# First stage of a four-layer graph network: scores earlier in TensorE's step, output projection two steps behind in fp32r parts

## The chip, the cores and the metric

The kernel runs on one core of one Trainium2 chip. The metric is the device time of one execution in microseconds. Engines named here: TensorE (PE, matrix products into PSUM banks), VectorE (DVE), ScalarE (ACT), GpSimd (POOL) and SyncE (SP, which issues the DMAs).

## The reference

Four graph layers over x [64, 128, 256] with one adjacency matrix of 128 x 128. Only the first matters here, attention with 8 heads of 32:

```python
h = jnp.maximum(_layernorm(x, axis=-1), 0.0)
q = split_heads(h @ Wq.T + bq)
k = split_heads(h @ Wk.T + bk)
v = split_heads(h @ Wv.T + bv)
scale = 1.0 / np.sqrt(D_HEAD)
scores = jnp.einsum('bhqd,bhkd->bhqk', q, k) * scale
scores = jnp.where(mask, -jnp.inf, scores)        # mask: adj == 0
attn = jax.nn.softmax(scores, axis=-1)
out = jnp.einsum('bhqk,bhkd->bhqd', attn, v)
x = x + out.transpose(0, 2, 1, 3).reshape(b, n, D_MODEL) @ Wo.T + bo
```

## The kernel before

The 64 graphs are taken in 32 groups of two (G = 2), and x stays in SBUF from the first layer to the last. Each layer is a stage of its own: a software pipeline over the groups, written by hand as one function per engine (`step0` to `step3`). `run_steps` calls such a function for steps -2, -1, 0, ... (the first and last ones written out, the middle in a hardware loop of two steps), and `at.group(lag)` gives the group that an engine handles in this step at a lag: `f` is the step's own group g, `b` the one before it, `n` the one after it. The order in each engine's queue is the order of the code; semaphores alone tie the engines together.

In a step of the first stage TensorE does, in this order: the q and k projections of group g (each 12 products of 256 columns, the inputs split into a high and a low fp32r part, three products for each pair, L1172); the transposes T0 and T1 of the first two blocks of probabilities of group g-1 (L1195; block r holds four heads' rows); the values of g (L1180); T2 and T3; the transposes of the normalised h of g+1 (L1160); the four mask products that fill banks 4 to 7 with -3e38 where there is no edge (L1224); the transposes of the widened reciprocal sums (L1229); the attention products of g-1 (32 short ones, L1237); the scores of g, added on the mask (L1246); and the output projection of g-1 in fp32 (L1259).

Bank 0 holds hT and the k projection, bank 1 the q projection and the values, bank 2 the transposes T0 and T2 and then the attention, bank 3 T1, T3, the sums and the output projection, banks 4 to 7 the scores. VectorE adds the k bias (kT, L591), copies T1 and T3 (L584), takes LayerNorm's statistics and moments for g+2 (L246, L261), the reciprocals (L602, L606), the low part hT_lo (L613), the attention times the reciprocals (att0T, L620), the four negated maxima (L625) with a small scaling behind each (L628), and adds the projection into x (L638). In steps 0 to 3 it also does a `late_part` each at the end of the step, weight preparation for later layers (L555 to L573), each instruction of which waits for the one before. ScalarE adds the q bias (L904), takes the exponentials (L894), copies T0 and T2 (L887), the values (L916) and the sums (L928), rounds hT_hi (L923) and normalises h (L289). GpSimd turns moments into scale and shift (L273 to L279) and adds the output bias into x (L302).

## Time and profile before

| | |
|---|---|
| median of 3 runs | 1662.28 us (1660.25 to 1665.63) |
| the profiled execution | 1662.14 us, its span 1660.3 us |
| TensorE, VectorE, ScalarE, GpSimd busy | 89%, 77%, 62%, 27% of the span |
| mean granted clock of TensorE | 0.965 of 2.4 GHz |
| first stage, last add into x ends | 459.4 us |

The span is counted from the first to the last instruction of the profiled execution. A timeline row gives start, length, engine, line and operation, what it writes and reads, and how often it stands there in a row; a bracket at its end is the idle time of the engine just before it, with what ended it. "PEclk" is the clock granted to TensorE, 1.00 for 2.4 GHz and 0.50 for 1.2 GHz. Matrix products overlap, so the distance from start to start is what one costs; the length of a row also holds the end of the last one. An fp32 product is recorded as two passes, so the four products of the output projection stand there as x8.

### The profile page before, as it was taken

The page shows a single profiled execution, that of the slowest core. Times are in us where ns is not written, and L with a number is a line of the kernel's source. Part 1 is how long each engine was busy: PE and PEld are TensorE (multiplying, and loading weights), DVE is VectorE, ACT ScalarE, POOL GpSimd, SP SyncE. Part 2 cuts the span into 40 slices and gives each one's busy share as a digit, 9 for nine tenths or more (in the row PEclk, how much of TensorE's full clock was granted, in tenths as well). Part 3 has the DMA queues.
Part 4 walks back from the last instruction along what each step waited for, and adds up shares of the span by engine and source line. Part 5 has one row for each costly group of instructions (what it writes and reads, how often), then busy time and mean ns, then how long its engine had stood idle before and what let it go on. Part 6 is the DMA issues. An engine that isn't in the chain of part 4 may idle for free.

```text
span 1660.3 us, 36159 instructions
## 1 busy us (share of the span) xinstructions
PE 1471.5 (89%) x11454; PEld 1242.8 (75%) x11517; DVE 1283.4 (77%) x3002; ACT 1021.6 (62%) x3208; POOL 440.7 (27%) x745
## 2 busy tenths in 40 slices
PE   5789999999879977999999999999999999975776
PEld 4678888888779965787877777787877778764554
DVE  4877777777567758788888888888888888754997
ACT  3568788788645546565666556565666656533776
POOL 1112212212046642031222223132222222122332
PEclk9899999999979988999999999999999999996999
DMA  7400000000000000000000000000000000000112
GB/s 235 133 2 0 0 0 0 0 0 0 1 1 0 0 0 1 1 1 1 0 0 0 0 0 0 0 0 0 0 0 0 0 0 1 1 1 7 64 63 70
DMA packets 23873, 24.22 MB, mean 15 GB/s; under 512 B 1936, under 2 KB 23184, under 8 KB 23696
## 3 DMA queue, kind: packets, MB, share of 16 engines
q1 hardware_dynamic: 23824, 23.60, 4.5%
q8 instruction: 26, 0.43, 0.1%
q14 instruction: 23, 0.19, 0.0%
HBM read 15.21 MB, written 8.39 MB: 14 GB/s over the span
## 4 chain that ended last, share of the span: by engine, by line
PE 42%; DVE 26%; ACT 18%; issue 11%; POOL 1%; DVEq 0%; DMA 0%; ACTq 0%; SPq 0%; POOLq 0%
ACT probs L894 9%; PE bank L1323 4%; PE bank L1436 4%; PE bank L1160 3%; DVE headsT_lo L695 3%; PE bank L1374 3%; DVE probs L706 3%; PE bank L1246 2%; DVE em L688 2%; PE bank L1389 2%; PE bank L1237 2%; ACT probs L1005 2%; PE bank L1278 2%; PE bank L1290 2%; PE bank L1291 2%
## 5 line engine op out<-in xcount | busy, mean ns | idle before, releaser
L894 ACT ACTIVATE probs<-bank,negtop 128x128 f32<-128x128 f32 x512 | 185.8, 415 | 47.6 <-DVE negtop L628 47.5
L273 POOL TENSOR_TENSOR var_eps<-mv,eps_tile 128x2 f32<-128x2 f32 x128 | 38.3, 299 | 636.6 <-DVE mv L261 636.6
L1330 PE MATMUL bank<-aggT_hi,wh_hi 128*128 128x256 f32 x512 | 148.5, 290 | 12.2 <-DVE em L690 9.2
L289 ACT ACTIVATE h<-x_all,shift,rstd 128x256 f32 (+1 forms) x256 | 139.9, 596 | 31.5 <-POOL shift L279 31.5
L1343 PE MATMUL bank<-wout_hi,headsT_hi 128*128 128x258 f32 x512 | 156.2, 305 | 0.0
L980 ACT CAST aggT_hi<-bank 128x512 fp32r<-128x512 f32 x128 | 75.2, 588 | 120.3 <-PE bank L1323 120.3
L1330 PE MATMUL bank<-aggT_lo,wh_hi 128*128 128x256 f32 x512 | 145.1, 283 | 0.0
L1330 PE MATMUL bank<-aggT_hi,wh_lo 128*128 128x256 f32 x512 | 145.1, 283 | 0.0
L1343 PE MATMUL bank<-wout_lo,headsT_hi 128*128 128x258 f32 x512 | 144.5, 282 | 0.0
L1343 PE MATMUL bank<-wout_hi,headsT_lo 128*128 128x258 f32 x512 | 144.2, 282 | 0.0
L1323 PE MATMUL bank<-probsT,h 128*128 128x512 f32 x256 | 133.2, 625 | 0.5 <-ACT probsT L1013 0.5
L894 ACT ACTIVATION_READ_ACCUMULATOR probs<-bank,negtop 128x1 f32 x512 | 130.1, 254 | 0.0
L485 POOL TENSOR_TENSOR var_y<-mv_y,eps_tile 128x2 f32<-128x2 f32 x32 | 6.3, 196 | 466.3 <-DVE mv_y L755 466.3
L695 DVE TENSOR_TENSOR headsT_lo<-em,headsT_hi 128x512 fp32r<-128x512 f32 x128 | 127.6, 1014 | 2.7 <-ACT headsT_hi L993 2.4
L993 ACT CAST headsT_hi<-em 128x512 fp32r<-128x512 f32 x128 | 79.1, 618 | 61.8 <-DVE em L690 61.8
L1330 PEld LDWEIGHTS bank<-aggT_hi,wh_hi 128*128 128x128 f32 x512 | 97.4, 190 | 19.4 <-DVE em L690 15.6
L275 POOL TENSOR_TENSOR rstd<-var_eps,pow_half 128x2 f32<-128x2 f32 x128 | 104.6, 817 | 10.0
L701 DVE TENSOR_TENSOR aggT_lo<-bank,aggT_hi 128x512 fp32r<-128x512 f32 x128 | 86.6, 677 | 24.2 <-ACT aggT_hi L980 24.1
L1195 PE MATMUL bank<-consts,probs 128*128 128x128 f32 x512 | 75.7, 281 | 31.7 <-DVE probsT L584 17.1
L1160 PE MATMUL bank<-consts,h 128*128 128x128 f32 x384 | 64.6, 295 | 43.0 <-ACT h L289 43.0
L1005 ACT ACTIVATE probs<-probs,negtop 128x128 f32<-128x128 f32 x256 | 99.4, 400 | 1.0 <-DVE negtop L708 1.0
L1343 PEld LDWEIGHTS bank<-wout_lo,headsT_hi 128*128 128x128 f32 x512 | 97.3, 190 | 1.0 <-issue 0.2
(209 smaller groups left out, 4718.2 us busy)
## 6 DMA issues: line engine op xcount, KB each, us to landing
x_all<-in_x SPq DMA_DIRECT2D x32, 256.0 KB, 2.8
out_x<-x_all SPq DMA_DIRECT2D x32, 256.0 KB, 2.1
wh<-in_L_gnn_W_heads SPq DMA_DIRECT2D x2, 512.0 KB, 7.7
a_heads<-in_L_gnn_a_heads SPq DMA_DIRECT2D x1, 1024.0 KB, 11.0
wout<-in_L_gnn_W_out SPq DMA_DIRECT2D x1, 1024.0 KB, 11.1
raw<-in_L_gnn_W SPq DMA_DIRECT2D x1, 512.0 KB, 5.6
ffn<-in_L_gnn_w SPq DMA_DIRECT2D x2, 256.0 KB, 7.1
consts<-in_shape_consts SPq DMA_DIRECT2D x1, 322.0 KB, 2.7
```

What stands on the lines that cost most here:

```text
L275: nc.gpsimd.tensor_tensor(rstd[:, p, :], var_eps[:, p, :], pow_half[:, :], ALU.pow).then_inc(s.norm, 1)
L289: last = nc.scalar.activation(h[:, p, c, :], x_all[:, bass.ds(g * G + c, 1), :].rearrange("p a d -> p (a d)"), ACT.Relu, bias=shift[:, p, ...
L695: nc.vector.tensor_tensor(headsT_lo[:, i].rearrange("p k c n -> p k (c n)"), em[:, i % 2], headsT_hi[:, i].rearrange("p k c n -> p k (c n) ...
L701: nc.vector.tensor_tensor(aggT_lo[:, dc, :, c, :], bank[3 + (2 + i) % 4][:, :].rearrange("p (h n) -> p h n", h=H2), aggT_hi[:, dc, :, c, : ...
L894: last = nc.scalar.activation(probs[:, r, i, :], bank[4 + r][:, i * N:(i + 1) * N], ACT.Exp, bias=negtop0[:, r, i:i + 1], scale=float(DH) ...
L993: nc.scalar.copy(headsT_hi[:, i].rearrange("p k c n -> p k (c n)"), em[:, i % 2]).then_inc(hd2_hi, 1)
L1005: last = nc.scalar.activation(probs[:, c, hh, :], probs[:, c, hh, :], ACT.Exp, bias=negtop2[:, c, hh:hh + 1], accum_out=sum2[:, c, hh:hh + 1])
L1160: last = nc.tensor.transpose(dst[:, (k * G + c) * N:(k * G + c + 1) * N], src[:, c, k * N:(k + 1) * N], ident)
L1195: last = nc.tensor.transpose(bank[2 + r % 2][:, k * N:(k + 1) * N], probs[:, r, k, :], ident)
L1323: nc.tensor.matmul(bank[3 + (2 + i) % 4][:, :], h[:, pm, c, dc * N:(dc + 1) * N], probsT[:, c].rearrange("p h n -> p (h n)"), start=True, ...
L1330: last = nc.tensor.matmul(bank[3 + i % 2][:, o * G * N:(o + 1) * G * N], w[:, k, i, o * N:(o + 1) * N], src[:, k, i].rearrange("p c n -> p ...
L1343: last = nc.tensor.matmul(bank[5 + c][:, 0:D + 2], src[:, i, o, c, :], w[:, k, :], start=(k == 0 and src is headsT_hi and w is wout_hi), s ...
```

## The change

- **Scores.** The mask products and the scores of g move from the end of TensorE's step to the place behind T0, T1 and T2, ahead of the values. VectorE's maxima 0 to 2 move up with them, the fourth goes near the end of VectorE's step; ScalarE takes exponentials 0, 1 and 2 in this step and the fourth in the next.
- **Output projection.** It handles group g-2 (`z`, lag 2) between the two halves of the k projection, writes bank 2, and is made of three fp32r products for each pair, out of att0T_hi, att0T_lo and woT_hi, woT_lo. VectorE makes att0T_hi and att0T_lo in each step, and the weights' parts once in the setup. The add into x is the first thing in VectorE's step, for g-2.
- **Scale.** The factor 32^-0.5 goes into q's activation (and into bq once), out of the exponential and out of the small scaling behind each maximum, which is dropped.
- **Third bank for transposes.** T2 goes to bank 1, T0, T1, T2 stand together, and T3 goes to bank 2 behind h's transposes; ScalarE copies T0 and T2, VectorE T1 and T3.
- **h.** ScalarE normalises h of g+1 in the step, not of g+2; the statistics for g+2 stand behind the attention on VectorE.

```diff
@@ block.vector, setup
+            nc.vector.tensor_scalar(bq_c[:, :], bq_c[:, :], float(DH) ** -0.5, None, ALU.mult)
...
+            nc.vector.tensor_copy(woT_hi[:, :, :], bank[3][:, :].rearrange("p (c o) -> p c o", c=2)).then_inc(weights_dve, 1)
+            dve.wait_ge(weights_dve, 6)
+            nc.vector.tensor_tensor(woT_lo[:, :, :], bank[3][:, :].rearrange("p (c o) -> p c o", c=2), woT_hi[:, :, :].bitcast(FP32),
+                                    ALU.subtract).then_inc(weights_dve, 1)
@@ block.vector, step0
+                if z:
+                    dve.wait_ge(o_full, gz + 1)
+                    dve.wait_ge(pre[0].bias, gz + 1)
+                    nc.vector.tensor_tensor(x_group(gz), bank[2][:, :].rearrange("p (c d) -> p c d", c=G), x_group(gz),
+                                            ALU.add).then_inc(pre[0].x, 1)
...
+                    nc.vector.tensor_tensor(att0T[:, :, :, :], bank[2][:, :].rearrange("p (k c n) -> p k c n", k=KC, c=G),
+                                            rsumT[:, :, :, :], ALU.mult).then_inc(aT_ready, 1)
+                    dve.wait_ge(aT_ready, gb * 3 + 1)
                     if positive(gb):
                         dve.wait_ge(o_full, gb)
-                    nc.vector.tensor_tensor(att0T[:, :, :, :], bank[2][:, :].rearrange("p (k c n) -> p k c n", k=KC, c=G),
-                                            rsumT[:, :, :, :], ALU.mult).then_inc(aT_ready, 1)
...
-                    dve.wait_ge(top0_step, g * 8 + 2 * r + 1)
-                    nc.vector.tensor_scalar(negtop0[:, r, :], negtop0[:, r, :], float(DH) ** -0.5, None, ALU.mult).then_inc(top0_step, 1)
...
+                    nc.vector.tensor_copy(att0T_hi[:, :, :, :], att0T[:, :, :, :]).then_inc(aT_ready, 1)
+                    dve.wait_ge(aT_ready, gb * 3 + 2)
+                    nc.vector.tensor_tensor(att0T_lo[:, :, :, :], att0T[:, :, :, :], att0T_hi[:, :, :, :].bitcast(FP32),
+                                            ALU.subtract).then_inc(aT_ready, 1)
+                pre_dve(dve, 0, at)
+                stats_written(dve, 0, at)
+                if f:
+                    top(3)
+                moments_dve(0, at)
@@ block.scalar, step0
                 if b:
-                    exp(2, gb, pb)
+                    exp(3, gb, pb)
                     probs_T(0)
-                    exp(3, gb, pb)
+                    probs_T(2)
@@ block.tensor, step0
                     project_T(bank[1], wqT_hi, wqT_lo).then_inc(q_full, 1)
-                    project_T(bank[0], wkT_hi, wkT_lo).then_inc(k_full, 1)
+                    project_T(bank[0], wkT_hi, wkT_lo, (0,))
+                if z:
+                    pe.wait_ge(aT_ready, gz * 3 + 3)
+                    for c in range(G):
+                        for k in range(KC):
+                            for src, w in ((att0T_hi, woT_hi), (att0T_hi, woT_lo), (att0T_lo, woT_hi)):
+                                last = nc.tensor.matmul(bank[2][:, c * D:(c + 1) * D], src[:, k, c, :], w[:, k, :],
...
-                if b:
-                    pe.wait_ge(aT_ready, gb + 1)
-                    for c in range(G):
-                        for k in range(KC):
-                            last = nc.tensor.matmul(bank[3][:, c * D:(c + 1) * D], att0T[:, k, c, :], woT[:, k, :],
-                                                    start=(k == 0), stop=(k == KC - 1))
-                    last.then_inc(o_full, 1)
```

On TensorE the order of one step (of those written out at the front), the first row of a group each (T1 left out in the second), is before:

```order
L1195 MATMUL bank2<-consts,probs 128x128 [waits aT_ready,p0_ready]
...
L1195 MATMUL bank3<-consts,probs 128x128 [waits x_done0,p0_ready]
...
L1180 MATMUL bank1<-wvT_hi,hT_hi 128x256 [waits q_ready]
...
L1195 MATMUL bank2<-consts,probs 128x128 [waits pT0_act,p0_ready]
...
L1195 MATMUL bank3<-consts,probs 128x128 [waits pT0_dve,p0_ready]
...
L1160 MATMUL bank0<-consts,h 128x128 [waits k_ready,h0]
...
L1224 MATMUL bank4<-hide0,ident_bf 128x512 [waits p0_ready]
...
L1229 MATMUL bank3<-consts,rwide0 128x128 [waits pT0_dve,rsum0_step]
...
L1237 MATMUL bank2<-probsT,v1 32x128 [waits pT0_act,v_ready]
...
L1246 MATMUL bank4<-kT,qT 128x128 [waits k_ready]
...
L1259 MATMUL bank3<-woT,att0T 128x256 [waits aT_ready]
...
L1172 MATMUL bank1<-hT_hi,wqT_hi 128x256 [waits v_ready,hT0_lo]
```

and after (line numbers of the changed kernel: L1184 projections, L1231 output projection, L1207 probabilities, L1245 masks, L1215 scores, L1192 values, L1171 h, L1276 attention):

```order
L1184 MATMUL bank1<-hT_hi,wqT_hi 128x256 [waits v_ready,hT0_lo]
...
L1231 MATMUL bank2<-woT_hi,att0T_hi 128x256 [waits aT_ready]
...
L1184 MATMUL bank0<-hT_hi,wkT_hi 128x256
...
L1207 MATMUL bank2<-consts,probs 128x128 [waits x_done0,p0_ready]
...
L1207 MATMUL bank1<-consts,probs 128x128 [waits q_ready,p0_ready]
...
L1245 MATMUL bank4<-hide0,ident_bf 128x512 [waits p0_ready]
...
L1215 MATMUL bank4<-kT,qT 128x128 [waits q_ready,k_ready]
...
L1192 MATMUL bank1<-wvT_hi,hT_hi 128x256 [waits pT0_act]
...
L1171 MATMUL bank0<-consts,h 128x128 [waits k_ready,h0]
...
L1207 MATMUL bank2<-consts,probs 128x128 [waits pT0_act,p0_ready]
...
L1266 MATMUL bank3<-consts,rwide0 128x128 [waits pT0_dve,rsum0_step]
...
L1276 MATMUL bank2<-probsT,v1 32x128 [waits pT0_dve,pT0_act,v_ready]
```

The masks and scores have moved from behind the attention to ahead of the values, and T3 from ahead of h's transposes to behind them; the sums' transposes and the attention products follow T3 directly. The output projection, once the last group of the step, stands between the halves of the k projection, and T0, which now waits for the add into x (x_done0), comes behind it.

On VectorE the same part of a step is before:

```order
L591 TENSOR_SCALAR kT<-bank0,bk_c 128x256 [waits s0_full,k_full,late_setup]
...
L584 COPY probsT<-bank3 128x512 [waits av_full,pT0_full]
L246 BN_STATS st<-x_all 128x6 [waits x_loaded1]
...
L602 RECIPROCAL rsum0<-sum0 128x16 [waits rT_full,p0_ready,stats0]
L261 BN_AGGR mv<-st 128x2 x2
L606 TENSOR_SCALAR rwide0<-rsum0,poison 128x512 [waits rsum0_step]
L584 COPY probsT<-bank3 128x512 [waits pT0_full]
L613 TENSOR_TENSOR hT_lo<-bank0,hT_hi 128x512 [waits hT0_hi]
L620 TENSOR_TENSOR att0T<-bank2,rsumT 128x512 [waits o_full,rT_ready,av_full]
L625 TENSOR_REDUCE negtop0<-bank4 128x4 [waits s0_full,p0_ready]
L628 TENSOR_SCALAR negtop0<-negtop0 128x4 [waits top0_step]
...
L638 TENSOR_TENSOR x_all<-bank3,x_all 128x512 [waits bias0,o_full]
```

and after (L602 the add into x, L609 kT, L592 copies of T1 and T3, L596 maxima, L633 hT_lo, L638 att0T):

```order
L602 TENSOR_TENSOR x_all<-bank2,x_all 128x512 [waits bias0,o_full,late_setup]
L609 TENSOR_SCALAR kT<-bank0,bk_c 128x256 [waits s0_full,k_full]
...
L592 COPY probsT<-bank3 128x512 [waits av_full,pT0_full]
L617 RECIPROCAL rsum0<-sum0 128x16 [waits rT_full,p0_ready]
L619 TENSOR_SCALAR rwide0<-rsum0,poison 128x512 [waits rsum0_step]
L596 TENSOR_REDUCE negtop0<-bank4 128x4 [waits s0_full,p0_ready]
...
L592 COPY probsT<-bank2 128x512 [waits pT0_full]
L633 TENSOR_TENSOR hT_lo<-bank0,hT_hi 128x512 [waits hT0_hi]
L638 TENSOR_TENSOR att0T<-bank2,rsumT 128x512 [waits rT_ready,av_full]
L643 CAST att0T_hi<-att0T 128x512 [waits o_full,aT_ready]
L645 TENSOR_TENSOR att0T_lo<-att0T,att0T_hi 128x512 [waits aT_ready]
L248 BN_STATS st<-x_all 128x6 [waits x_loaded1]
```

The add into x has gone from the end of the step to its front, where it waits for the projection (o_full) and stands ahead of kT. The maxima stand ahead of the copy of T3, and two more operations, att0T_hi and att0T_lo, follow att0T ahead of the statistics (BN_STATS).

## Rows read from the trace of the kernel before

**Rows 1.** Busy time of each engine in one window, a steady step.

```profile
core 0: us, PE busy (x) PEld busy (x) DVE busy (x) ACT busy (x) POOL busy (x), PEclk, DMA share, GB/s
232.40:244.80 12.40, 11.96 (x137) 10.64 (x137) 8.79 (x21) 10.02 (x42) 2.78 (x5) 1.00 0.00 0
```

**Rows 2.** Waits from 108 to 404 us: total us, times, longest us.

```profile
PE bank L1195 <- ACT probs L894: 9.3, 24, 0.4
```

**Rows 3.** Timeline of TensorE, one steady step: start us, us, what it runs.

```profile
232.39 0.47 PE L1172 MATMUL bank<-hT_hi,wqT_hi 128*128 128x256 f32 x1
232.69 0.28 PE L1172 MATMUL bank<-hT_hi,wqT_lo 128*128 128x256 f32 x1
...
235.44 1.04 PE L1195 MATMUL bank<-consts,probs 128*128 128x128 f32 x8
236.23 0.36 PE L1180 MATMUL bank<-wvT_hi,hT_hi 128*128 128x256 f32 x1
...
237.75 0.60 PE L1195 MATMUL bank<-consts,probs 128*128 128x128 f32 x4
238.74 0.66 PE L1195 MATMUL bank<-consts,probs 128*128 128x128 f32 x4 [0.39 <-ACT probs L894]
239.23 0.60 PE L1160 MATMUL bank<-consts,h 128*128 128x128 f32 x4
...
240.53 0.60 PE L1229 MATMUL bank<-consts,rwide 128*128 128x128 f32 x4
241.06 1.08 PE L1237 MATMUL bank<-probsT,v 128*32 128x128 f32 x32
242.07 1.17 PE L1246 MATMUL bank<-kT,qT 32*128 32x128 f32 x32
243.17 1.99 PE L1259 MATMUL bank<-woT,att0T 128*128 128x256 f32 x8
244.82 0.47 PE L1172 MATMUL bank<-hT_hi,wqT_hi 128*128 128x256 f32 x1
```

**Rows 4.** Timeline of VectorE, the same step.

```profile
243.26 0.69 DVE L625 TENSOR_REDUCE negtop<-bank 128x4 f32<-128x512 f32 x1 [0.36 <-PE bank L1246]
...
244.09 0.69 DVE L625 TENSOR_REDUCE negtop<-bank 128x4 f32<-128x512 f32 x1
...
248.96 0.68 DVE L584 COPY probsT<-bank 128x512 f32<-128x512 f32 x1
```

**Rows 5.** Line 638, the add into x: count, then minimum, median, maximum in ns.

```profile
L638 DVEq FUSED_REGOPS  x26: 71/71/71, 109.8 to 420.6; - x26
```

**Rows 6.** Timelines of VectorE and TensorE in steps 2 and 3, around a late part.

```profile
61.86 0.88 DVE L591 TENSOR_SCALAR kT<-bank,bk_c 128x256 f32<-128x256 f32 x2
...
72.93 0.69 DVE L638 TENSOR_TENSOR x_all<-bank,x_all 128x512 f32<-128x512 f32 x1
73.53 0.68 DVE L563 TENSOR_TENSOR prod<-wh,a_heads 128x512 f32<-128x512 f32 x1
...
79.32 0.88 DVE L591 TENSOR_SCALAR kT<-bank,bk_c 128x256 f32<-128x256 f32 x2
...
80.94 1.09 PE L1195 MATMUL bank<-consts,probs 128*128 128x128 f32 x4 [3.76 <-DVE probsT L584]
```

**Rows 7.** Windows behind TensorE's restart in step 3.

```profile
80.90:82.90 2.00, 1.94 (x8) 1.85 (x10) 1.93 (x7) 0.00 (x0) 0.90 (x2) 0.50 0.00 0
84.90:86.90 2.00, 2.00 (x64) 1.69 (x64) 0.69 (x1) 1.57 (x3) 0.15 (x1) 1.00 0.03 8
```

**Rows 8.** Lines 688 and 695, second GNN stage: minimum, median, maximum in ns.

```profile
L688 DVE TENSOR_SCALAR em<-em x128: 411/420/1123, 644.2 to 1462.9; 128x512 f32<-128x512 f32 x128
...
L695 DVE TENSOR_TENSOR headsT_lo<-em,headsT_hi x128: 676/682/1790, 647.0 to 1465.6; 128x512 fp32r<-128x512 f32 x128
```

**Rows 9.** Timeline of VectorE in the setup.

```profile
18.01 0.42 DVE L536 TENSOR_TENSOR bo_row<-bank,bo_row 128x256 f32<-128x256 f32 x1 [0.44 <-PE bank L1152]
```

**Rows 10.** Timeline of TensorE, end of the first stage.

```profile
454.87 3.78 PE L1259 MATMUL bank<-woT,att0T 128*128 128x256 f32 x8 [0.81 <-DVE att0T L620]
```

More of the change, by code:

```diff
@@ L183, in build_program @@
                 woT = sb_0("woT", [N, KC, D])
+                woT_hi, woT_lo = [sb_0(f"woT_{part}", [N, KC, D], F32R) for part in ("hi", "lo")]
                 hT_hi = sb_0("hT_hi", [N, KC, G, N], F32R)
@@ L190, in build_program @@
                 att0T = sb_0("att0T", [N, KC, G, N])
+                att0T_hi, att0T_lo = [sb_0(f"att0T_{part}", [N, KC, G, N], F32R) for part in ("hi", "lo")]
             with ExitStack() as layer1:
@@ L1166, in step0, with project_T @@
                 b, gb, pb = at.group(1)
-                def project_T(dst, w_hi, w_lo):
-                    for o in range(KC):
+                z, gz, _ = at.group(2)
+                def project_T(dst, w_hi, w_lo, parts=(0, 1)):
+                    for o in parts:
                         for k in range(KC):
@@ new lines, in step0 @@
+                if f:
+                    project_T(bank[0], wkT_hi, wkT_lo, (1,)).then_inc(k_full, 1)
+                if b:
+                    probs_T(0)
+                    probs_T(1)
+                    probs_T(2)
+                if f:
+                    for r in range(4):
+                        if positive(g):
+                            pe.wait_ge(p0_ready, g * 4 - 3 + r)
+                        nc.tensor.matmul(bank[4 + r][:, :], ident_bf[:, :], hide0[:, :, :], start=True, stop=False)
@@ new lines, in step0 @@
+                if b:
+                    pe.wait_ge(v_ready, gb + 1)
+                    pe.wait_ge(pT0_act, gb * 2 + 2)
+                    pe.wait_ge(pT0_dve, gb * 2 + 2)
+                    for k in range(KC):
+                        for c in range(G):
+                            i = k * G + c
+                            for r in range(4):
+                                last = nc.tensor.matmul(bank[2][r * DH:(r + 1) * DH, i * N:(i + 1) * N], v1[:, pb, c, k * 4 + r, :],
+                                                        probsT[:, r, i, :], start=True, stop=True)
+                    last.then_inc(av_full, 1)
```

147 lines of the change are left out of this document (62 added, 85 removed).

## The prediction

> **What bounds the kernel now.** The change touches the first stage alone, the attention layer, which runs from the setup to 459.4 us. I read it in this order. First one step in windows: in 12.40 us TensorE is busy for 11.96, ScalarE for 10.02, VectorE for 8.79, at the full granted clock of 2.4 GHz [rows 1]. So TensorE's own work nearly fills the step. Then the waits of 24 steps: TensorE waits in one place for another engine, for the exponentials ahead of the transpose of the fourth block of probabilities, 9.3 us in all, 0.39 a step [rows 2]. Then its timeline gives the step: 232.39 to 244.82, that is 12.43 us, cut into pieces by the starts of the groups [rows 3]. Two things should be seen there. A 256-column fp32r product follows the one before it after 0.12 us (23 of them from 232.69 to 235.44); the first behind fp32 work takes 0.30. And the four fp32 products of the output projection (eight passes) take 1.65. Last the steps of the fill: VectorE has a late part to do in steps 0 to 3 (weight preparation of later layers, 5.8 us in step 2), and the steps there are 17.46 us long, from one kT to the next (61.86 to 79.32) [rows 6].
>
> **TensorE's own work after.** The projection becomes 12 fp32r products in the middle of fp32r work: 12 x 0.12 = 1.43 instead of 1.65, a gain of 0.22. The wait of 0.39 ahead of T3 goes: T3 now stands behind scores and values, long after the fourth exponential. T2 took 0.99 with that wait, 0.60 without; in one row of transposes it should take 0.40, as T0 and T1 do (0.79 for both), a gain of 0.20. T3 takes 0.49 after its wait and should take 0.40, and the transposes of the sums behind it 0.40 instead of 0.53 (the mask products no longer stand in front). The first q product now follows the short attention products, not the fp32 projection, about -0.10. The scores inherit the place behind the mask products, +0.09. Sum: 12.43 - 0.22 - 0.39 - 0.20 - 0.09 - 0.13 - 0.10 + 0.09 = 11.39 us, if nothing waits.
>
> **What is late next, in the steady steps.** Two waits come in, by the order of after and the durations of before. (1) T0 writes bank 2, which the projection of two steps back has just filled, so T0 waits for VectorE's add into x. The projection's last product ends 0.16 behind the next issue (0.28 against 0.12 in [rows 3]), the semaphore takes 0.03 (243.24 to 243.26 from the scores to the first maximum [rows 3, 4]), VectorE's address registers for x_all come behind the wait and take 0.07 in the loop [rows 5], the add is 0.69 [rows 6], 0.06 more on both sides: 1.01. The second half of the k projection covers 0.71. Wait 0.30, and 0.1 for the restart (T3 shows 0.49 against 0.40). (2) The attention products need the fourth block copied by VectorE. T3's end, 0.16 + 0.03, the copy 0.68 [rows 4], 0.03: 0.90, of which the sums' transposes cover 0.40. Wait 0.50. Step: 11.39 + 0.40 + 0.50 = 12.29, say 12.3 us. Against 12.43 this is -0.13, and over 27 steady steps -3.5 us.
>
> **VectorE and ScalarE in the steady step.** VectorE loses four scalings: maximum to maximum is 0.83 [rows 4], to become 0.61, so -0.9. It gains the copy att0T_hi and the difference att0T_lo. Neither is in the trace. For the difference the nearest row is headsT_lo, two SBUF sources of 128x512, median 0.68, maximum 1.79 [rows 8]; I take 0.69. For the copy the nearest is the one-source operation on em in SBUF, median 0.42 [rows 8]; the other end is 0.69, as a copy out of PSUM takes. I take 0.43. Then from the end of the attention products: 0.14, multiply 0.69, copy 0.43, difference 0.69 and two gaps of 0.04, that is 2.06 us into the next step, and TensorE wants it at 1.53 + 0.71 = 2.24. Covered by 0.18; with the copy at 0.69 a wait of 0.08. Behind them stand the statistics, the fourth maximum and the moments, which end near 3.4, before the projection does (3.8). The Trainium skill, VectorE: DVE Perf Modes, section "The perf-mode tier table", gives an fp32 tensor_copy in SBUF the double rate and a tensor_tensor the single one; by that rule the sum stays as it is, and if the copy fell out of it (0.69) some 2 us would be added. No row here shows whether an fp32r output keeps the double rate. ScalarE has the same work in another order; its next maximum is there before it is free, or it waits 1.2 us with nothing behind that TensorE needs. The scale folded into q costs nothing there, since the same instruction carries it. The normalised h is made one step later than before, at about 6.5 us into the step, for transposes at 9.4.
>
> **The fill.** This is where the change loses. Setup: two more operations with PSUM sources, 0.6 each from start to start (as 72.93 to 73.53 [rows 6]), and the small scaling of bq on VectorE, less the 0.44 that it idles there now [rows 9]: +0.8. In steps 2, 3 and 4 the add into x will be the first thing on VectorE, behind the late part of the step before. Today kT comes there and TensorE's T3 waits 3.76 us for the next copy [rows 6]; then it works at 1.2 GHz for some 3 to 4 us (clock 0.50 in the window from 80.90, 1.00 in that from 84.90 [rows 7]). After the change the chain from the late part is: add 0.6; T0, T1, T2 at the low clock 2.4 to 2.6; masks 1.3 to 1.7; scores 1.1; that is 5.6. Then values, h's transposes and T3 2.4, tail 0.2, copy 0.7, attention products 1.1, multiply, copy and difference 1.8, statistics, fourth maximum and moments 1.5: 13.3 us ahead of the next late part. Today it is 17.46 less the late part (73.53 to 79.32, 5.8) = 11.7. So +1.6 in each of two steps and half as much in the one behind step 3: +4. Steps 0 and 1 I take as even, since there is no projection yet.
>
> **The drain.** At half clock the last projection takes 3.78 [rows 10], twice what it takes in the steady step; as 12 fp32r products at twice 0.12 it takes 2.9. The copy and difference in front of it cost 1.2, its gain is 0.9: even, within the 1 us or so that the other waits there may shift.
>
> **Sum.** -3.5 + 0.8 + 4 + 0 = +1.3 us on the profiled execution's 1662.14 (span 1660.3), which stands at the median of the runs, 1662.28. I forecast 1663 us. Within 0.3%, 5 us, is what a measurement of this kernel can't tell from no change.
>
> **Rivals.** (A) Faster: the waits cost less than I put on them, or TensorE's groups lie closer. For it speaks that the bare work falls to 11.39 and VectorE's idle time is ample (3.6 us of 12.4). Each 0.1 us less of a step is 2.7 us; with the two waits at 0.5 instead of 0.9 the step is 11.9, -0.53 x 27 = -14, and with setup and fill at +5 the time is 1653. Against it: both waits are chains of known operations. Chance 0.25. (B) Slower, by the difference att0T_lo. The nearest operations mostly take 0.68, but some take up to 1.79 [rows 8]. If the difference takes 1.0 here, by whatever holds those up, and the copy 0.69, the chain is 2.61 instead of 2.06, TensorE waits 0.4 for the projection, and the step is 12.7: 27 x 0.27 = +7, with setup and fill +5 and their own four steps +2: 1676. It decides from a chain of 2.2 us on. Against it: GpSimd's norm and bias work starts when the moments are done, near 3.4 us into the step, when the difference is over. Chance 0.13. The Trainium skill, SBUF — State Buffer, section "Who interferes with whom", has the rule behind it: a VectorE instruction with two SBUF inputs and a GpSimd one that reads SBUF exclude each other for the whole instruction; it would give this rival's time only if the two overlap. (C) Slower, by the clock in the fill. After a late part TensorE restarts today with eight transposes and four masks, and the clock is back within some 4 us of the restart (0.50, then 1.00, [rows 7]). After the change it restarts with 12 transposes, later in VectorE's chain; if the clock comes back later there, scores and values run at 1.2 GHz too, 1.1 + 1.5 us more in each of three steps at the worst, 1671, and 1667 at the half. For it speaks only that the idle time ahead is longer, 5 us against 3.76. Chance 0.12. (D) The change does what it says and the gain and the loss cancel: my forecast, 0.50, its own range 1657 to 1668.
>
> **Range and chances.** The step may be 12.1 to 12.5 (-9 to +2), the fill and setup +3 to +7, the drain -1 to +2. With the rivals the range is 1652 to 1673. Faster by over 0.3%: 0.25 (A). Within: 0.51. Slower by over 0.3%: 0.24 (B, most of C and a little of D).
>
> **What would show it.** In the steady steps of after: a period of 12.3; T0 waiting about 0.3 for x_all; the attention products waiting about 0.5 for probsT; the projection's 12 products in 1.43 us with no wait ahead of them; att0T_hi at 0.43. In steps 2 and 3: a period near 19 us, with TensorE idle for 5 us ahead of T0. The prediction is wrong if the attention products don't wait, or if the fill's steps stay near 17.5 us.

## The result: 0.9% slower

The changed kernel takes 1678.08 us (median of 4 runs, 1676.88 to 1679.08) against 1663.95 us for the kernel before on the same chip. The ratio is 1.0088, its 95% interval 1.0066 to 1.0109. I had forecast 1663 us and a range up to 1673.

Nearly the whole of it lies in the first stage. In the profiled executions its last add into x ends at 475.06 us instead of 459.38; what follows takes 1201.7 us instead of 1200.9. Cut at the kT of steps 0, 5 and 31, from VectorE's timeline:

| stretch | before | after | difference | forecast |
|---|---|---|---|---|
| start to kT of step 0 | 30.14 | 31.61 | +1.5 | +0.8 |
| kT 0 to kT 5 (fill) | 81.31 | 89.04 | +7.7 | +4 |
| kT 5 to kT 31 (26 steady steps) | 323.08 | 330.25 | +7.2 | -3.4 |
| kT 31 to the last add's end (drain) | 24.85 | 24.16 | -0.7 | 0 |

The steady steps, as a window of one of them (us; busy time of TensorE, its weight loads, VectorE, ScalarE, GpSimd; granted clock) and as TensorE's waits from 108 to 404 us. This is the view of [rows 1, 2]:

```profile
242.04:254.73 12.69, 11.93 (x139) 10.61 (x141) 9.39 (x20) 10.15 (x42) 2.51 (x5) 1.00 0.00 0
```

```profile
PE bank L1276 <- ACT v L938: 10.1, 23, 0.4
PE bank L1207 <- DVE x_all L602: 6.6, 23, 0.3
PE bank L1245 <- issue: 0.2, 1, 0.2
```

The period is 12.71 us (mean of the 20 steps from kT 8 to kT 28, as everywhere below), where it was 12.43. TensorE's busy time has not moved (11.93, was 11.96), and the one wait of 0.39 has become two, of 0.44 and 0.29. The view puts the first down to ScalarE's v. Its timeline and VectorE's correct that:

```profile
251.29 0.39 PE L1192 MATMUL bank<-wvT_hi,hT_hi 128*128 128x256 f32 x1
...
252.82 0.60 PE L1171 MATMUL bank<-consts,h 128*128 128x128 f32 x4
253.26 0.60 PE L1207 MATMUL bank<-consts,probs 128*128 128x128 f32 x4
253.69 0.60 PE L1266 MATMUL bank<-consts,rwide 128*128 128x128 f32 x4
254.73 1.08 PE L1276 MATMUL bank<-probsT,v 128*32 128x128 f32 x32 [0.44 <-ACT v L938]
```

```profile
243.18 0.69 DVE L638 TENSOR_TENSOR att0T<-bank,rsumT 128x512 f32<-128x512 f32 x1 [0.69 <-PE bank L1276]
243.90 0.43 DVE L643 CAST att0T_hi<-att0T 128x512 fp32r<-128x512 f32 x1
244.36 0.69 DVE L645 TENSOR_TENSOR att0T_lo<-att0T,att0T_hi 128x512 fp32r<-128x512 f32 x1
...
253.89 0.69 DVE L592 COPY probsT<-bank 128x512 f32<-128x512 f32 x1 [0.63 <-PE bank L1207]
```

The attention products need the v of a step ago (the code waits for `gb + 1`), which was copied long before. VectorE's copy of T3 ends at 253.89 + 0.69 = 254.58, 0.15 ahead of them: that is the wait I had foreseen. In a_scale, one of the experiments below, the same view names that copy (probsT, 10.1 us, 23 times) and not v. The other place, T0 behind the output projection, in the same step:

```profile
245.30 0.28 PE L1231 MATMUL bank<-woT_hi,att0T_hi 128*128 128x256 f32 x1
...
246.74 0.28 PE L1184 MATMUL bank<-hT_hi,wkT_hi 128*128 128x256 f32 x1
...
247.34 0.28 PE L1184 MATMUL bank<-hT_lo,wkT_hi 128*128 128x256 f32 x1
...
247.89 1.50 PE L1207 MATMUL bank<-consts,probs 128*128 128x128 f32 x12 [0.27 <-DVE x_all L602]
```

The 12 fp32r products take 246.74 - 245.30 = 1.44 us and nothing waits ahead of them. T0 starts 0.55 behind the last k product instead of 0.12, so its wait costs 0.43 with the restart.

The fill, in the view of [rows 6]: VectorE and GpSimd at the end of step 1 with the start of the next late part, and TensorE's restart in step 3 (the first of its four mask products is missing in the record):

```profile
60.44 0.69 DVE L571 TENSOR_REDUCE wh_f<-prod 128x2 f32<-128x512 f32 x1
61.16 1.33 DVE L570 TENSOR_TENSOR prod<-wh,a_heads 128x512 f32<-128x512 f32 x1
...
78.34 0.66 DVE L570 TENSOR_TENSOR prod<-wh,a_heads 128x512 f32<-128x512 f32 x1
```

```profile
60.68 1.26 POOL L304 TENSOR_TENSOR x_all<-x_all,bo_row 128x512 f32<-128x512 f32 x1
```

```profile
85.57 2.79 PE L1207 MATMUL bank<-consts,probs 128*128 128x128 f32 x12 [6.12 <-DVE x_all L602]
88.59 1.06 PE L1245 MATMUL bank<-hide,ident_bf 128*128 128x512 bf16 x3 [0.22 <-issue]
89.58 1.17 PE L1215 MATMUL bank<-kT,qT 32*128 32x128 f32 x32
```

TensorE idles for 6.12 us ahead of T0 (3.76 in [rows 6]) and restarts at half clock: 3.02 us from T0 to the first recorded mask product. One operation of the late part takes 1.33 us instead of 0.69: it starts while GpSimd adds the output bias (60.68 to 61.94), and ends 0.55 behind it. The same happens in step 2 (81.20, beside an addition from 80.72 to 81.98).

### The profile page after: what moved, and what is told of

Its sections match the earlier page's. It is cut to its first block, busy times and chain, and to the rows that moved or that the text cites. A ratio compares the mean times of both kernels' runs of the same rounds, so it can differ in the third digit from the quotient of the medians.

```text
span 1676.8 us, 36577 instructions
## 1 busy us (share of the span) xinstructions
PE 1468.7 (88%) x11582; PEld 1241.9 (74%) x11645; DVE 1304.4 (78%) x2941; ACT 1024.1 (61%) x3208; POOL 437.3 (26%) x745
## 4 chain that ended last, share of the span: by engine, by line
PE 48%; DVE 28%; ACT 12%; issue 10%; POOL 1%; DVEq 1%; DMA 0%; SPq 0%; ACTq 0%; POOLq 0%
PE bank L1340 4%; PE bank L1184 4%; PE bank L1453 4%; DVE headsT_lo L707 3%; PE bank L1391 3%; PE bank L1207 3%; PE bank L1231 3%; PE bank L1171 3%; DVE probs L718 3%; ACT probs L906 2%; PE bank L1215 2%; DVE em L700 2%; PE bank L1406 2%; PE bank L1276 2%; PE bank L1309 2%
## 5 line engine op out<-in xcount | busy, mean ns | idle before, releaser
L906 ACT ACTIVATE probs<-bank,negtop 128x128 f32<-128x128 f32 x512 | 182.2, 400 | 64.5 <-DVE negtop L596 64.5
L275 POOL TENSOR_TENSOR var_eps<-mv,eps_tile 128x2 f32<-128x2 f32 x128 | 33.9, 265 | 655.6 <-DVE mv L263 655.6
L906 ACT ACTIVATION_READ_ACCUMULATOR probs<-bank,negtop 128x1 f32 x512 | 122.3, 239 | 0.0
L596 DVE TENSOR_REDUCE negtop<-bank 128x4 f32<-128x512 f32 x128 | 82.5, 686 | 38.1 <-PE bank L1215 34.8
L1171 PE MATMUL bank<-consts,h 128*128 128x128 f32 x384 | 62.3, 287 | 43.8 <-ACT h L291 43.8
```

The source lines that it names most:

```text
L596: nc.vector.tensor_reduce(negtop0[:, r, :], bank[4 + r][:, :].rearrange("p (k n) -> p k n", k=4), AX.X, ALU.max, negate=True).then_inc(top ...
L906: last = nc.scalar.activation(probs[:, r, i, :], bank[4 + r][:, i * N:(i + 1) * N], ACT.Exp, bias=negtop0[:, r, i:i + 1], accum_out=sum0[: ...
L1171: last = nc.tensor.transpose(dst[:, (k * G + c) * N:(k * G + c + 1) * N], src[:, c, k * N:(k + 1) * N], ident)
```

## The experiments

Twelve kernels besides the changed one; the fill is from kT 0 to kT 5 as in the table above. The ratio is to the kernel before on the same chip. Fill and step come from one profiled execution each.

| kernel | us | ratio (95% interval) | fill | steady step |
|---|---|---|---|---|
| after | 1678.1 | 1.0088 (1.0066 to 1.0109) | 89.0 | 12.71 |
| a_late | 1670.8 | 1.0048 (1.0032 to 1.0064) | 59.0 | 12.71 |
| b_late | 1662.6 | 1.0005 (0.9994 to 1.0015) | 58.6 | 12.43 |
| a_t3 | 1665.8 | 1.0020 (1.0008 to 1.0032) | 89.5 | 12.31 |
| a_t1t3 | 1654.0 | 0.9944 (0.9923 to 0.9965) | 86.9 | 11.86 |
| a_nobias | 1678.1 | 1.0113 (1.0093 to 1.0134) | 88.0 | 12.71 |
| a_proj32 | 1681.2 | 1.0130 (1.0111 to 1.0149) | 88.4 | 13.06 |
| a_scale | 1683.2 | 1.0142 (1.0121 to 1.0164) | 92.0 | 12.80 |
| a_bank | 1688.1 | 1.0170 (1.0148 to 1.0192) | 91.4 | 13.17 |
| a_split | 1662.5 | 1.0018 (1.0006 to 1.0030) | 76.2 | 12.71 |
| b_split | 1651.6 | 0.9949 (0.9929 to 0.9968) | 71.4 | 12.41 |
| a_t1t3s | 1637.8 | 0.9862 (0.9841 to 0.9883) | 73.9 | 11.86 |
| a_best | 1634.0 | 0.9845 (0.9827 to 0.9864) | 74.7 | 11.83 |

The rest of the program behind the first stage took between 1198.5 and 1204.6 us in these profiles (1226.6 and 1223.6 in a_late and b_late, which do the late parts there), so differences of 3 us between single times say little; the periods say more.

**The two waits: a_t3 and a_t1t3.** T3 goes ahead of h's transposes:

```diff
                     values(1).then_inc(v_full, 1)
+                if b:
+                    probs_T(3)
                 n, gn, pn = at.group(-1)
 ...
                     transpose_group(bank[0], h[:, pn]).then_inc(hT0_full, 1)
                 if b:
-                    probs_T(3)
                     pe.wait_ge(rsum0_step, gb * 2 + 2)
```

> The changed kernel with the transpose T3 ahead of h's transposes instead of behind them, so that h's transposes (0.44 us) too lie between T3 and the attention products. Theory (the attention products wait some 0.5 us for VectorE's copy of T3, and this wait is on the path of the steady step): the wait goes, 0.4 to 0.5 us a step, the period falls from 12.71 to 12.25 to 12.35 us, and the whole takes 11 to 13 us less than the changed kernel, about 1666. Rival (the step is set by a loop through VectorE or ScalarE, and TensorE's waits are only where the slack shows): the wait moves to another group, to h's transposes or the next q projection, and the period stays above 12.6.

The period fell by 0.40, to 12.31, so the rival, a loop through another engine, is out. In a_t1t3 T1 stands ahead of T0 too (with the counts of pT0_full that the others wait for):

```diff
                 if b:
-                    probs_T(0)
                     probs_T(1)
+                    probs_T(0)
                     probs_T(2)
```

> As a_t3, and T1 ahead of T0 as well, since T1 goes to bank 3 and needs no add into x. Theory: T1 (0.44 us) covers the wait for the add too (0.4 us with the restart), and the step is TensorE's bare work of some 11.8 us; the whole is 22 to 25 us less than the changed kernel, about 1654, which is below the kernel before. Rival (a loop through VectorE): VectorE now starts the copy of T1 before kT, no gain over a_t3, or less than 0.1 us a step.

Another 0.45: the period is 11.86, and the change with its two waits covered beats the kernel before. TensorE's timeline of one step, which is now its bare work:

```profile
241.18 0.60 PE L1207 MATMUL bank<-consts,probs 128*128 128x128 f32 x4
241.61 0.60 PE L1171 MATMUL bank<-consts,h 128*128 128x128 f32 x4
242.05 0.60 PE L1267 MATMUL bank<-consts,rwide 128*128 128x128 f32 x4
242.65 1.08 PE L1277 MATMUL bank<-probsT,v 128*32 128x128 f32 x32
243.66 0.38 PE L1184 MATMUL bank<-hT_hi,wqT_hi 128*128 128x256 f32 x1
...
248.10 1.51 PE L1207 MATMUL bank<-consts,probs 128*128 128x128 f32 x12
249.45 1.03 PE L1245 MATMUL bank<-hide,ident_bf 128*128 128x512 bf16 x4
```

T0 to T2 take 1.35 us, T3 and h's transposes 0.44 each, and the sums' transposes 0.60, with no wait recorded. I had put 1.19, 0.40 and 0.40 on T0 to T2, T3 and the sums. The restart costs more than the idle time that the waits' view shows for it: T0's wait stands there with 0.29, and covering it brought 0.45.

**The fill: a_late and b_late.** In both kernels the four late parts go behind the first stage:

```diff
-                if isinstance(at.t, int) and 0 <= at.t < 4:
-                    late_part(at.t)
             run_steps(dve, NG, step0)
+            for i in range(4):
+                late_part(i)
```

> The changed kernel with its four late parts taken out of steps 0 to 3 and done in a row behind the first stage. Read from kT of step 0 to kT of step 5: the kernel before has 81.3 us there, the changed one 89.0; five steady steps of the changed kernel would be 63.5. Theory (the late part stands ahead of the add into x and so of T0, and its chain is longer): without late parts the five steps take 64 to 67 us, some 22 to 25 less, and the first stage's last add into x ends near 452. Rival (the fill is slower because groups are in flight for longer, whatever VectorE has to do beside them): 70 us or more. The late parts then stand between the stages, so about 24 us come back there and the whole time is within 5 us of the changed kernel's 1678.

> The kernel before with its four late parts done in a row behind the first stage in the same way. From kT of step 0 to kT of step 5 it now takes 81.3 us; five steady steps are 62.2. Theory: 62 to 66 us without late parts, so that the two kernels differ there by no more than the 1.4 us of their steady steps and what the setup gives. Rival (the changed order loses its 7.7 us in the fill without the late parts too): this one gains 16 us or more and the changed one gains less than that, so that they stay 5 us or more apart.

The fill is 59.0 and 58.6 us, less than either theory asked; steps 0 and 1 are shorter than a steady step there (8.8 and 12.2 us in a_late). Without late parts the orders differ by 0.4 us, less than the 1.4 that five steady steps alone would give; with them by 7.7. So the loss in the fill comes from the late parts and what follows from their place. One thing that follows is the clock: from 30 to 100 us it is 1.00 in both kernels, while the kernel before and the changed one have four stretches at 0.50 in their fills. The kernel before gained nothing in all (its 22.7 us came back behind the stage), the changed one 7, more than the 5 that I had allowed (its first stage ended at 442 us, where I had 452); that is the extra that its fill had lost.

**Why the late part grew: a_nobias.** GpSimd's bias addition in the first stage is cut to 4 columns of each 256, so the rest of x lacks the output bias:

```diff
-            nc.gpsimd.tensor_tensor(x_group(g), x_group(g), row[:, :, :].broadcast_to([N, G, D]), ALU.add).then_inc(pre[k].bias, 1)
+            cut = slice(0, 4) if k == 0 else slice(0, D)
+            nc.gpsimd.tensor_tensor(x_group(g)[:, :, cut], x_group(g)[:, :, cut], row[:, :, cut].broadcast_to([N, G, cut.stop]), ALU.add).then_inc(pre[k].bias, 1)
```

> The changed kernel with GpSimd's addition of the output bias in the first stage cut to 4 columns of each 256 (so the rest of x lacks the output bias), and the same instruction otherwise. In the trace of the changed kernel one operation of the late part in steps 0, 1 and 2 starts while GpSimd adds the bias and takes 1.33 us instead of 0.69, or 2.34 instead of 1.23 (two SBUF sources of VectorE against GpSimd); before the change the bias addition fell elsewhere. Theory (that overlap is what made the late parts longer): those three operations return to 0.69 and 1.23, and from kT of step 0 to kT of step 5 the kernel takes 2 to 2.7 us less than 89.0; the steady period stays 12.71; the whole is 2 to 3 us less than 1678. Rival (the long operations are held up by something else, a DMA or the weights' arrival): they stay long and the time stays.

That the bias addition makes the late part's operations longer is shown. The same operations in steps 0 and 1 (VectorE's timeline):

```profile
39.07 1.26 DVE L576 TENSOR_TENSOR prod<-wout,em 128x1024 f32<-128x1024 f32 x1
...
58.50 0.69 DVE L571 TENSOR_TENSOR prod<-wh,a_heads 128x512 f32<-128x512 f32 x1
```

They were 2.34 and 1.33. The price in all is not what I expected: the fill fell by 1.0, not 2 to 2.7, and the whole did not gain. The steps from kT to kT tell where it went:

| step | 0 | 1 | 2 | 3 | 4 |
|---|---|---|---|---|---|
| before | 13.81 | 17.91 | 17.46 | 18.73 | 13.39 |
| after | 14.90 | 18.80 | 20.04 | 21.11 | 14.19 |
| a_nobias | 13.82 | 17.88 | 20.05 | 21.74 | 14.55 |

Steps 0 and 1 are back at the times of the kernel before, 2.0 us less, so their loss came with the overlap. Step 2 gained nothing, and steps 3 and 4 lost 1.0. In a_nobias T0 of step 3 starts again after 5.49 us of idle:

```profile
82.29 2.79 PE L1208 MATMUL bank<-consts,probs 128*128 128x128 f32 x12 [5.49 <-DVE x_all L603]
85.31 1.49 PE L1246 MATMUL bank<-hide,ident_bf 128*128 128x512 bf16 x3 [0.22 <-issue]
86.72 1.36 PE L1216 MATMUL bank<-kT,qT 32*128 32x128 f32 x32
```

From T0 to the scores it takes 4.43 us, in the changed kernel 4.01. The stretch at half clock around this restart, first in a_nobias, then in the changed kernel, with the sum of all four such stretches of the fill under each (the clock is the third column from the end):

```profile
80.34:87.16 6.82, 4.65 (x23) 3.45 (x28) 3.86 (x8) 2.16 (x4) 0.00 (x0) 0.50 0.00 0
sum 23.88, PE 15.68 PEld 12.90 DVE 14.67 ACT 7.18 POOL 0.00; mean PE 3.92 PEld 3.23 DVE 3.67 ACT 1.80 POOL 0.00
```

```profile
82.27:89.09 6.82, 3.29 (x14) 2.92 (x16) 5.14 (x10) 1.27 (x3) 0.00 (x0) 0.50 0.00 0
sum 27.30, PE 13.05 PEld 12.28 DVE 21.02 ACT 3.97 POOL 0.83; mean PE 3.26 PEld 3.07 DVE 5.26 ACT 0.99 POOL 0.21
```

Full speed is back 4.9 us behind T0 in a_nobias and 3.5 us behind it in the changed kernel, so more of TensorE's work fell into the slow stretch. The output projection takes 3.78 us at half clock against 1.99 [rows 3, 10]; by that, as an estimate, slow work costs half its length. In the four stretches, which end in steps 1 to 4, a_nobias has 3.42, 4.22, 4.65 and 3.39 us of it, the changed kernel 4.11, 2.85, 3.29 and 2.79. Half of each difference, and the 1.1, 0.64 and 0.64 us that the late parts of steps 0 to 2 became shorter, make -1.1, -1.0, 0.0, +0.7 and +0.3 for steps 0 to 4; measured are -1.1, -0.9, 0.0, +0.6 and +0.4. So the clock accounts for what was lost again, though no run holds it fixed. Time saved ahead of a restart was in part lost behind it. When the clock comes back after a restart I can't tell beforehand from these traces.

**The late parts in pieces: a_t1t3s, b_split, a_split.** Each late part becomes a generator that yields after each product and sum, and is called up in four places of VectorE's step; for the changed orders:

```diff
+                next(ops, None)
                 if f:
 ...
                     top(2)
+                next(ops, None)
 ...
+                next(ops, None)
                 pre_dve(dve, 0, at)
 ...
-                if isinstance(at.t, int) and 0 <= at.t < 4:
-                    late_part(at.t)
+                for _ in ops:
+                    pass
```

> The kernel a_t1t3 (T1 ahead of T0, T3 ahead of h's transposes) with each late part cut into three or four pieces that stand ahead of the first maximum, behind the third, ahead of the statistics and at the end of VectorE's step, instead of in one piece at the end. a_t1t3 takes 86.9 us from kT of step 0 to kT of step 5, of which five steady steps would be 59.3. Theory (what costs is the one block of 5.8 to 7 us ahead of the add into x, with TensorE idle and then slow): pieces lie in part in VectorE's own idle time, a step of the fill is 15 to 17 us, the five steps take 74 to 80 us, and the whole 7 to 12 us less than a_t1t3, 1642 to 1647. Rival (VectorE's sum of work is what counts in the fill, wherever it stands, or each piece holds up the chain in turn): 84 us or more, and the whole within 3 us of 1654.

> The kernel before with its late parts cut in the same way (behind the statistics, behind the copy of T3, ahead of the maxima and at the end). It takes 81.3 us from kT of step 0 to kT of step 5. If pieces help both orders alike, 74 to 78 us here and the whole 4 to 7 us less than the kernel before; if the block hurts only where the add into x stands behind it, 80 us or more and the same time as before within 2 us.

> The changed kernel in its own order on TensorE, with each late part cut into pieces as in a_t1t3s. Theory (block and order are independent): the same 12 to 17 us off as a_t1t3s had from a_t1t3, so 1661 to 1666, no longer slower than the kernel before as it stands, but 10 to 14 us slower than the kernel before with its late parts cut (1651.6): 27 steady steps at 0.28 us, 7.6, and some 3 to 5 that the setup and the longer chain cost in the fill. Rival (the changed order loses nothing once the block is gone): within 5 us of 1651.6.

The pieces take 13.0 us off the fill of a_t1t3, 12.9 off that of the changed kernel and 9.9 off that of the kernel before: the block hurts every order, the changed one by 3 us more. How much of this is the clock is not separated. TensorE's work in stretches at half clock falls with the pieces from 15.1 us to 2.9 in the kernel before, from 13.1 to 8.6 in the changed one and from 14.7 to 9.2 in a_t1t3; by the same estimate that is 6, 2 and 3 us. In the changed kernel the three late operations stretched by GpSimd, 2.4 us, are at their short times too. My expectation of b_split, 74 to 78, was too careful, and so was that of a_t1t3s by some 4 us. In step 2 of a_t1t3s VectorE has no idle time left ahead of the maxima (1.7 in the same place of the changed kernel):

```profile
61.43 0.68 DVE L571 TENSOR_TENSOR prod<-wh,a_heads 128x512 f32<-128x512 f32 x1
62.15 0.69 DVE L572 TENSOR_REDUCE wh_f<-prod 128x2 f32<-128x512 f32 x1
62.88 1.89 DVE L599 TENSOR_REDUCE negtop<-bank 128x4 f32<-128x512 f32 x3
64.68 0.68 DVE L571 TENSOR_TENSOR prod<-wh,a_heads 128x512 f32<-128x512 f32 x1
```

a_split against b_split, 1662.5 to 1651.6, keeps the 0.3 us a step (12.71 against 12.41) and 4.8 us of the fill, of which 1.5 are that 0.3 in five steps; TensorE's slow work (8.6 against 2.9 us) may hold most of the rest, but no run separates it.

**The parts one by one: a_proj32, a_scale, a_bank.** Each takes one part of the change back. The projection in fp32 at its new place, without att0T_hi and att0T_lo:

```diff
-                            for src, w in ((att0T_hi, woT_hi), (att0T_hi, woT_lo), (att0T_lo, woT_hi)):
-                                last = nc.tensor.matmul(bank[2][:, c * D:(c + 1) * D], src[:, k, c, :], w[:, k, :],
+                            last = nc.tensor.matmul(bank[2][:, c * D:(c + 1) * D], att0T[:, k, c, :], woT[:, k, :],
```

> The changed kernel with the output projection as it was, four fp32 products out of att0T and woT, at its new place, and with neither att0T_hi nor att0T_lo. Theory (three fp32r products gain their 0.2 us on TensorE, and VectorE's copy and difference, 1.12 us, cost the steady step nothing but lengthen the fill's chain): the steady period rises from 12.71 to 12.9 to 13.0 us (+5 to +8 us), the five steps from kT of step 0 to kT of step 5 fall by 2 to 4 us, and the whole lies 2 to 5 us above the changed kernel. Rival (the copy and the difference are on the path of the steady step too): the period falls below 12.7 and the whole below 1675.

The period rose by 0.35, more than I expected of this run, which left out what the fp32r product behind the fp32 ones costs. TensorE's timeline shows both halves of it:

```profile
233.56 1.89 PE L1225 MATMUL bank<-woT,att0T 128*128 128x256 f32 x8
235.10 0.47 PE L1179 MATMUL bank<-hT_hi,wkT_hi 128*128 128x256 f32 x1
235.41 0.28 PE L1179 MATMUL bank<-hT_hi,wkT_lo 128*128 128x256 f32 x1
```

1.54 for the products, and 0.31 for the first fp32r product behind them, where the changed kernel has 1.44 and 0.12: 0.29 more in all. The fill fell by 0.6 only, not by 2 to 4. TensorE idled for less ahead of T0 of step 3 (4.67 us, not 6.12), but 17.8 us of its work fell into stretches at half clock instead of 13.1; by the estimate above that is 2.4 us lost again.

The scale back in the exponential and in four small scalings:

```diff
-                                                    bias=negtop0[:, r, i:i + 1],
+                                                    bias=negtop0[:, r, i:i + 1], scale=float(DH) ** -0.5,
 ...
+                    dve.wait_ge(top0_step, g * 8 + 2 * r + 1)
+                    nc.vector.tensor_scalar(negtop0[:, r, :], negtop0[:, r, :], float(DH) ** -0.5, None, ALU.mult).then_inc(top0_step, 1)
```

> The changed kernel with the scale put back where it was: in the exponential and in a small scaling behind each of the four maxima, and not in q nor in bq. Theory (VectorE has slack in the steady step: it stood idle for 0.37 us ahead of the add into x, and only the fourth maximum's scaling, 0.22 us, lies ahead of that add): the steady period stays at 12.71 to 12.75 us; in the fill, where VectorE is the chain, four scalings a step cost 2 to 3.5 us over four steps; the whole is 2 to 5 us above 1678. Rival (VectorE is on the path of the steady step as well): the period rises by 0.2 us or more and the whole by 7 or more.

Period +0.09, a little above the bound, and fill +3.0 as expected. In every second step the moments behind the fourth scaling end only with the projection, and the add into x starts 0.39 us behind the projection's end instead of 0.16. So this part is worth 2.3 us in the steady steps. For the fill the 3.0 is not shown to be the scalings' own: step 2 alone grew by 1.6 us, more than four scalings of 0.22 each, and 17.0 us of TensorE's work stood at half clock instead of 13.1.

T2 in bank 2 again (ScalarE's copy of T2 reads it there, and the values no longer wait for that copy):

```diff
-                    if r == 2 and f:
-                        pe.wait_ge(q_ready, g + 1)
-                    if r == 3:
+                    if r == 2:
                         pe.wait_ge(pT0_act, gb * 2 + 1)
+                    if r == 3:
+                        pe.wait_ge(pT0_act, gb * 2 + 2)
 ...
-                        last = nc.tensor.transpose(bank[(2, 3, 1, 2)[r]][:, k * N:(k + 1) * N], probs[:, r, k, :], ident)
+                        last = nc.tensor.transpose(bank[(2, 3, 2, 2)[r]][:, k * N:(k + 1) * N], probs[:, r, k, :], ident)
```

> The changed kernel without the third bank: T2 goes to bank 2 again, behind ScalarE's copy of T0, all else as it is (T0, T1 and T2 still in a row). Theory: ScalarE starts its copy 0.2 us behind T0's end and takes 0.6, T1 covers 0.44, so T2 waits 0.4 to 0.5 us with its restart; the period rises to 13.1 to 13.2 us and the whole to 1688 to 1692. Rival (something else is behind T0 to T2 anyway, such as kT for the scores): the wait is absorbed there and the period stays below 12.9.

```profile
240.25 1.07 PE L1207 MATMUL bank<-consts,probs 128*128 128x128 f32 x8 [0.30 <-DVE x_all L602]
241.55 0.66 PE L1207 MATMUL bank<-consts,probs 128*128 128x128 f32 x4 [0.24 <-ACT probsT L899]
```

T2 starts 1.30 behind T0 instead of 0.9, and the period is 13.17, +0.46. The third bank is worth 12 us in the 26 steady steps once T0 to T2 stand in a row.

**The best version: a_best.** a_t1t3s with T3 behind the scores, and the output weights' parts made in step -1:

```diff
                     scores(0)
                     scores(1)
+                if b:
+                    probs_T(3)
 ...
+                if isinstance(at.t, int) and at.t == -1:
+                    nc.vector.tensor_copy(woT_hi[:, :, :], woT[:, :, :]).then_inc(weights_dve, 1)
+                    dve.wait_ge(weights_dve, 6)
+                    nc.vector.tensor_tensor(woT_lo[:, :, :], woT[:, :, :], woT_hi[:, :, :].bitcast(FP32), ALU.subtract).then_inc(weights_dve, 1)
```

> a_t1t3s with two more edits. T3 stands directly behind the scores, ahead of the values; and the high and low parts of the output weights are made at the end of VectorE's step -1, where it idles, out of woT in SBUF, instead of in the setup. In a_t1t3 the attention products start 0.60 us behind the sums' transposes, 0.15 behind the end of VectorE's copy of T3. Theory (a rest of that wait is still in it): with the copy long done it is 0.50 to 0.55, the period 11.77 to 11.82 instead of 11.86, and kT of step 0 stands 0.8 to 1.3 us earlier; the whole 2 to 4 us below 1637.8. Rival (0.60 is what attention products cost behind fp32 transposes, with no wait in it): the period stays 11.86 and only the setup's 1 us shows.

```profile
239.17 0.60 PE L1276 MATMUL bank<-consts,rwide 128*128 128x128 f32 x4
239.70 1.08 PE L1286 MATMUL bank<-probsT,v 128*32 128x128 f32 x32
...
242.99 0.36 PE L1240 MATMUL bank<-woT_hi,att0T_hi 128*128 128x256 f32 x1
243.19 0.28 PE L1240 MATMUL bank<-woT_lo,att0T_hi 128*128 128x256 f32 x1
```

Sums to attention products is 0.53: 0.07 of the 0.60 was a rest of the wait, 0.53 is what they cost, as in [rows 3]. Half of the gain is gone at once: att0T_lo ends at 242.91, and the projection now starts right behind it, with 0.20 instead of 0.12 to its second product. The period is 11.83. kT of step 0 stands at 28.78, 1.6 us earlier than in a_t1t3s, of which a part is scatter (below). Its fill is 0.8 us longer than that of a_t1t3s, with 12.6 us of TensorE's work at half clock instead of 9.2. It is the fastest version, 1.55% below the kernel before.

## Why the prediction was wrong

**The step that failed: "TensorE's own work after", 11.39 us.** With both waits covered it measured 11.86, 0.47 more. The step's other half, the waits at 0.90, measured 0.43 and 0.44, together 0.87. So the forecast of 12.3 became 12.71 by one sum of small terms, read from group starts:
- T0 to T2 were to take 0.79 + 0.40 and took 1.35. The 0.79 of [rows 3] ends where the first value product starts, and that product then takes 0.21 to its second instead of 0.12: part of the transposes' cost stood behind the boundary. Four transposes among transposes cost 0.44, not 0.40.
- The sums' transposes were to fall from 0.53 to 0.40, on the argument that the masks no longer stand in front. They took 0.60, and 0.53 with the wait removed. The 0.53 is what lies ahead of the attention products, not behind the masks. This term had the wrong cause and is the largest error, 0.13 and 0.07. (Counted against 0.53, the wait for T3's copy costs 0.51, which is what I had put on it, and the bare work is 11.79.)
- T3 took 0.44 instead of 0.40, the projection's start and the rest 0.07 more.

At 26 steps 0.41 us too little is 11 us, most of the 15 by which I missed; the fill has 4 of the rest. The measured 1678 lies outside my 1652 to 1673 for these two reasons, and none of my rivals (A) to (C) names the first.

**Right:** T0's wait (0.40 forecast, 0.43 measured); the wait for T3's copy (0.50, 0.44), which a_t3 shows to be the copy's and not v's; 12 products in 1.44 us with no wait ahead; att0T_hi at 0.43 and att0T_lo at 0.69, in all 32 steps, so rival (B) is out. The chain to att0T_lo ended 2.01 us into the step (2.06 forecast; my terms add up to 2.03), and TensorE wanted it at 2.25 (2.24). The Trainium skill, VectorE: DVE Perf Modes, section "The perf-mode tier table": its double rate for an fp32 copy in SBUF holds here with an fp32r output too, 0.43 us, and 0.40 for woT_hi in a_best.

**The gain of the new projection** was right in size: 1.65 became 1.44, and the first q product behind it takes 0.22 to the next instead of 0.31. Together that is 0.30, and a_proj32, which takes the projection back at its new place, loses 0.35.

**The fill, forecast +4, measured +7.7: the second step that failed.** Steps 0 and 1, which I had called even, grew by 1.1 and 0.9: there GpSimd's bias addition falls into the late part, one operation takes 2.34 us instead of 1.23 and one 1.33 instead of 0.69, and a_nobias, without the overlap, gives these two steps the times of the kernel before. Step 2 grew by 2.6 us, not 1.6: the chain from the late part on took 64.69 to 78.34, 13.65 (13.3 forecast, against 11.7 before), and the late part itself 6.4 instead of 5.8, by the same overlap. Step 3 grew by 2.4, nearly all in the chain, 13.87 against 11.56; its late part was not stretched. Step 4 grew by 0.8, as forecast. The Trainium skill, SBUF — State Buffer, section "Who interferes with whom", has the rule for the overlap, and I had applied it to att0T_lo alone; this trace agrees with it for the late part: the two-source operation that starts 0.48 us behind the addition ends 0.55 us after it, and with the addition cut short it takes 0.69. Rival (C), the clock, did not decide: full speed was back 3.5 us behind T0 of step 3, within the 4 that I had assumed, and over the fill 13.1 us of TensorE's work stood at half clock, against 15.1 in the kernel before (the sum of its four stretches between 43.2 and 104.6 us). But a_nobias and a_proj32 show that it can move one or two microseconds.

**The setup** grew by 1.5 in these two profiles. But kT of step 0 stands anywhere from 30.13 to 31.61 in the nine kernels with the changed setup (mean 30.7) and from 29.51 to 30.53 in the three with the setup of before (mean 30.1): +0.6. That agrees with the forecast's 0.8, but the scatter of a microsecond allows other values as well.

**The drain** was even within 0.7 us, as forecast within 1 us.

## What to carry to other kernels

When a step is rearranged on a full engine, sum its new work from pieces that include their boundaries: add up start to start of whole rows, and see on which side of a boundary the cost stands (here 0.47 us in 11.4). A step that gives up one wait of 0.39 for two of 0.43 and 0.44 has gained nothing; look for a piece without that dependency to put between producer and consumer, as T1 ahead of T0 (0.45 us) and T3 ahead of h (0.40 us) were, before judging the order. A long block on a helper engine at the end of a step is priced by what stands first in the next: cut it up, and note also which engine's work it will now overlap. Where TensorE restarts at half clock, do not book microseconds saved ahead of the restart in full: of 2.0 us saved in a_nobias 1.0 stayed.

## What I had not expected of the hardware

- An operation of VectorE with two SBUF sources that starts while GpSimd adds 128x512 elements in SBUF (1.26 us) ends 0.55 us after it, and one of 128x1024 (40.36 to 42.70, beside an addition from 40.34 to 41.62) 1.08 after it: 1.33 instead of 0.69 us, and 2.34 instead of 1.23. With the addition cut to 4 columns both are gone. When VectorE's operation starts first, it is GpSimd that takes longer: in step 3 one of VectorE's from 101.08 to 102.31 kept its 1.23 us, and the addition that started at 101.30 took 2.13. With one source in PSUM and one in SBUF neither is stretched: in the kernel before hT_lo runs beside the addition 17 times (48.16 and 48.23, for one), at 0.69 us, the addition at 1.27 to 1.29.
- After similar idle times (6.12 and 5.49 us) the clock was back at 1.00 3.5 and 4.9 us behind T0, and TensorE's work from T0 to the scores took 4.01 and 4.43 us: the return of the clock differs by more than a microsecond between otherwise like restarts.
- Four fp32 products of 256 columns behind fp32r work cost 1.54 us and 0.19 more at the next fp32r product (a_proj32); behind the short fp32 score products they cost 1.65 [rows 3].
